# Xattn and six transformer layers on one core: two value stationaries per head, norm sums in SBUF, new slot orders

## Chip, cores and metric

The kernel runs on 1 core of one Trainium2 chip. The metric is device time in microseconds: the median of 3 runs.

## What is computed

Input x is 32 sequences of 128 tokens by 128 features, all fp32. First comes one cross attention (16 heads of 8, 4 key heads) with a residual. Then six layers of windowed attention and FFN, 192 pairs of (layer, sequence), which the kernel calls units. The part that the change is about, cut from the reference:

```python
def local_attention(q, k, v):          # 16 heads of 64, windows of 32
    bk2, bv2 = (look(bk), look(bv))    # each window sees the one before and itself
    mask = (it < jb) | (it > jb + w) | (jb == -1)
    sim = jnp.einsum('bhwie,bhwje->bhwij', bq, bk2) * QK_SCALE
    sim = jnp.where(mask, -jnp.finfo(sim.dtype).max, sim)
    attn = jax.nn.softmax(sim, -1)
    out = jnp.einsum('bhwij,bhwje->bhwie', attn, bv2)

def attn_layer(x, Wqkv, qs, ksc, Wo):
    q = l2norm(q) * qs; k = l2norm(k) * ksc      # per head
    q = q * cos * scale + rotate_half(q) * sin * scale
    k = k * cos * inv + rotate_half(k) * sin * inv
    return local_attention(q, k, v) @ Wo

def ffn_layer(x, g, bln, W1, b1, W2, b2):
    xn = (x - mu) / jnp.sqrt(var + 1e-05) * g + bln
    a, gate = jnp.split(xn @ W1 + b1, 2, -1)
    return a * gelu(gate) @ W2 + b2

for i in range(6):
    x = attn_layer(shift_tokens(x), ...) + x
    x = ffn_layer(shift_tokens(x), ...) + x
```

`shift_tokens` moves the second half of the features one token on.

## The kernel before, in words

Every engine runs its own program, written by hand as a list of steps with semaphore waits. The cross attention goes through 32 sequences in `xslot`. After that all engines go through `slot(n)`. In slot n TensorE, VectorE, ScalarE and GpSimd work on several units at once, each at its stage of the pipeline: unit n+2 is copied in, n+1 is transposed (`transpose_z`), unit n is projected to q, k and v and rotated, n-1 is normalized, n-2 has its heads transposed and its scores made, n-3 goes through softmax, P transposes and attend, n-4 through the output product (`attn_out`), the middle residual `z_mid`, the second norm and the first FFN product, n-5 through the last one. The order of the calls at the end of each engine's `slot` is the order of the work; there is no scheduler.

All data and products are fp32, so a product is two passes on TensorE (two instructions in the trace). The steps of TensorE in order: `attn_out` (L1363), `ffn_out` (L1351), `proj_qk(1)` (L1252), `transpose_qk` (L1290, 64 transposes of 32 rows), `transpose_z` (L1377), `proj_qk(2)` and `(3)`, `transpose_P` (L1270), `scores` (mask writes L1314, 64 products L1322), `attend` (48 products L1339), `transpose_zn` (L1383), `proj_v(0)` (L1262), `ffn_gate` (L1392), `ffn_a` (L1400), `proj_qk(0)`, `proj_v(1)`.

PSUM has eight banks. Banks 0 and 1 take the six projections of 512 columns in turn: each is squared and rotated (`rotary`, L963 and L966 on VectorE, into ta and tb) before the next may write. GpSimd adds ta and tb (L524) and multiplies by the norms rn (L533). Banks 2 to 5 take the head transposes; banks 2 and 3 (`SC`) also take the scores, and hold between them the sums of squares, the steps of the root (L976, L979, L982) and the row sums (L1075). So `transpose_qk` waits for `d_rn` (L985) and `d_rec`:

```python
wait(pe, "g_qk", count(4, b, 4))
wait(pe, "d_rn", count(1, m, 1))
wait(pe, "d_sub", count(2, b - 1, 2))
wait(pe, "d_rec", count(1, b - 1, 1))
```

Values are copied to vt (L705). The SP queue then makes the three overlapping shifts of them, vs, by DMA (`shift_v`, L351, six DMAs of a unit), and the one-token shift of zm (`shift_z`, L356). The statistics of the second norm (L1009) wait for that one. SP also loads the next layer's weights, in one fixed order. At the end of a layer this is `load_b2` (waits for the last zmb of GpSimd, L548), `shift_v(end + 2)`, `load_w1`, and then the first `shift_z` of the new layer.

## Time and profile before

| | |
|---|---|
| runs, us | 3307.62, 3308.11, 3310.73; median 3308.11 |
| profiled execution | span 3304.7 us (of this execution the span is what is known) |
| median less that span | 3.4 us |
| TensorE busy | 3125.4 us, 95% |
| VectorE, ScalarE, GpSimd busy | 87%, 81%, 74% |
| mean granted clock of TensorE | 0.978 |
| first transposed z of the layers | 302.3 us |
| last one | 3209.3 us |

The profile is of one execution. Busy time of TensorE overlaps, since a matmul's duration contains its way through the array; the distance between starts tells what a block costs. Idle time of an engine that nobody waits for costs nothing.

### The profile page before, as it was taken

The page shows a single profiled execution, that of the slowest core. Times are in us where ns is not written, and L with a number is a line of the kernel's source. Part 1 is how long each engine was busy: PE and PEld are TensorE (multiplying, and loading weights), DVE is VectorE, ACT ScalarE, POOL GpSimd, SP SyncE. Part 2 cuts the span into 40 slices and gives each one's busy share as a digit, 9 for nine tenths or more (in the row PEclk, how much of TensorE's full clock was granted, in tenths as well). Part 3 has the DMA queues.
Part 4 walks back from the last instruction along what each step waited for, and adds up shares of the span by engine and source line. Part 5 has one row for each costly group of instructions (what it writes and reads, how often), then busy time and mean ns, then how long its engine had stood idle before and what let it go on. Part 6 is the DMA issues. An engine that isn't in the chain of part 4 may idle for free.

```text
span 3304.7 us, 181505 instructions
## 1 busy us (share of the span) xinstructions
PE 3125.4 (95%) x71268; PEld 2192.5 (66%) x71268; DVE 2884.0 (87%) x6045; ACT 2663.4 (81%) x5440; POOL 2447.9 (74%) x2673
## 2 busy tenths in 40 slices
PE   6776899999999999999999999999999999999996
PEld 4443567676667676676767667676676767667665
DVE  7886789999899999899999899998899999899984
ACT  6886678888788888788888788888788888788874
POOL 3333778888788888788888778787787878788883
PEclk9988999999999999999999999999999999999997
DMA  3000112122222222222222212122221212212121
GB/s 79 8 7 10 47 51 59 50 59 71 67 56 53 56 53 77 63 54 55 54 55 74 68 50 59 50 59 77 57 59 50 59 50 77 66 50 59 50 58 50
DMA packets 150374, 182.24 MB, mean 55 GB/s; under 512 B 51572, under 2 KB 74162, under 8 KB 149554
## 3 DMA queue, kind: packets, MB, share of 16 engines
q1 hardware_dynamic: 150322, 181.55, 21.2%
q8 instruction: 33, 0.54, 0.1%
q14 instruction: 19, 0.16, 0.0%
HBM read 21.32 MB, written 2.10 MB: 7 GB/s over the span
## 4 chain that ended last, share of the span: by engine, by line
PE 57%; issue 13%; DVE 10%; ACT 10%; POOL 5%; SPq 1%; DVEq 1%; DMA 1%; ACTq 1%; POOLq 0%
PE bank L1252 13%; PE bank L1339 8%; PE bank L1322 7%; PE bank L1262 5%; PE bank L1363 5%; PE bank L1270 3%; PE bank L1290 3%; ACT L798 3%; DVE tb L966 3%; ACT P L774 3%; PE bank L1392 2%; ACT gl L766 2%; POOL qk L524 2%; DVE bank L1075 2%; PE bank L1400 2%
## 5 line engine op out<-in xcount | busy, mean ns | idle before, releaser
L533 POOL TENSOR_TENSOR qk<-qk,rn 128x512 f32<-128x512 f32 x768 | 803.0, 1046 | 356.8 <-DVE rn L985 356.8
L524 POOL TENSOR_TENSOR qk<-ta,tb 128x512 f32<-128x512 f32 x768 | 978.6, 1274 | 2.5 <-DVE tb L966 2.5
L1252 PE MATMUL bank<-wqkv,zsT 128*128 128x512 f32 x1536 | 819.9, 617 | 25.4 <-ACT vt L705 12.3
L963 DVE TENSOR_TENSOR ta<-bank,rot 128x512 f32<-128x512 f32 x768 | 527.5, 687 | 116.1 <-ACT sq L688 87.4
L966 DVE TENSOR_TENSOR tb<-bank,rot 128x512 f32<-128x512 f32 x768 | 523.0, 681 | 0.0
L1068 DVE TENSOR_REDUCE bank<-sq 128x32 f32<-128x2048 f32 x192 | 440.6, 2295 | 25.1
L688 ACT ACTIVATE sq<-bank 128x512 f32<-128x512 f32 x768 | 445.2, 611 | 14.8 <-PE bank L1252 12.1
L696 ACT ACTIVATE qkT<-bank 128x512 f32<-128x512 f32 x768 | 396.6, 602 | 57.1 <-PE bank L1290 56.9
L1363 PEld LDWEIGHTS bank<-wo,oT 128*128 128x128 f32 x3072 | 375.4, 193 | 92.4 <-issue 92.4
L743 ACT ACTIVATE znT<-bank,small 128x128 f32<-128x128 f32 x192 | 87.9, 458 | 431.8 <-PE bank L1383 431.8
L564 POOL TENSOR_TENSOR P<-P,rowsum 128x512 f32<-128x512 f32 x384 | 392.9, 1045 | 20.0 <-DVE rowsum L1083 20.0
L1262 PE MATMUL bank<-wqkv,zsT 128*128 128x512 f32 x768 | 399.8, 603 | 1.2 <-DVE tb L966 1.1
L1363 PE MATMUL bank<-wo,oT 128*128 128x128 f32 x3072 | 376.6, 276 | 0.5 <-ACT gl L766 0.5
L1252 PEld LDWEIGHTS bank<-wqkv,zsT 128*128 128x128 f32 x1536 | 238.0, 195 | 193.1 <-DVE tb L966 170.2
L1290 PEld LDWEIGHTS bank<-cst,qk 32*128 32x128 f32 x12288 | 212.5, 137 | 172.9 <-issue 172.9
L1339 PE MATMUL bank<-PT,vs 64*64 64x32 f32 (+1 forms) x18432 | 310.9, 220 | 11.3 <-issue 11.3
L1339 PEld LDWEIGHTS bank<-PT,vs 64*64 64x64 f32 x18432 | 291.4, 135 | 30.0 <-issue 12.3
L539 POOL TENSOR_TENSOR rstd<-ve,half_neg 128x1 f32<-128x1 f32 x192 | 105.8, 551 | 254.5 <-DVE ve L1023 254.5
L1075 DVE TENSOR_REDUCE bank<-P 128x16 f32<-128x1024 f32 x192 | 235.8, 1228 | 66.7 <-ACT P L774 66.6
L1322 PEld LDWEIGHTS bank<-qkT 64*32 64x32 f32 x24576 | 278.1, 105 | 14.1 <-issue 3.9
L1322 PE MATMUL bank<-qkT 64*32 64x64 f32 x24576 | 281.7, 225 | 3.0 <-issue 3.0
L1290 PE MATMUL bank<-cst,qk 32*128 32x32 f32 x12288 | 228.5, 223 | 21.0 <-DVE rowsum L1083 2.9
(131 smaller groups left out, 5740.6 us busy)
## 6 DMA issues: line engine op xcount, KB each, us to landing
vs<-vt SPq DMA_DIRECT2D x1152, 128.0 KB, 2.4
wqkv<-L_ffn_Wqkv SPq DMA_DIRECT2D x6, 1024.0 KB, 5.0
zm<-zm SPq DMA_DIRECT2D x192, 31.8 KB
wqkv<-L_ffn_Wqkv SPq DMA_DIRECT2D x6, 512.0 KB, 3.7
wo<-L_ffn_Wo SPq DMA_DIRECT2D x6, 512.0 KB, 4.0
z_sb<-x SPq DMA_DIRECT2D x4, 512.0 KB, 5.1
ctxb<-ctx SPq DMA_DIRECT2D x32, 64.0 KB, 1.8
w<-L_ffn_W SPq DMA_DIRECT2D x6, 341.0 KB
```

What stands on the lines that cost most here:

```text
L524: g.tensor_tensor(o, i0, i1, ALU.add).then_inc(s["g_add"], 1)
L533: g.tensor_tensor(q3, q3, r3, ALU.mult).then_inc(s["g_qk"], 1)
L688: a_.activation(sq[:, 512 * j:512 * j + 512], bank[j % 2][:, :], ACT.Square)\
L963: v_.tensor_tensor(ta[:, c].rearrange("p (h d) -> p h d", d=DH), bank[j % 2][:, :].rearrange("p (h d) -> p h d", d=DH), rot[:, o:o + 64].u ...
L966: v_.tensor_tensor(tb[:, c].rearrange("p (h c d) -> p h c d", c=2, d=32)[:, :, ::-1, :], bank[j % 2][:, :].rearrange("p (h c d) -> p h c d ...
L1068: v_.tensor_reduce(sm, sq[:, :].rearrange("p (h d) -> p h d", d=DH), AX.X, ALU.add)\
L1252: t_.matmul(bank[j % 2][:, :], zsT[:, pu, :], wqkv[:, 512 * j:512 * j + 512], start=True, stop=True).then_inc(s["p_qk"], 1)
L1262: t_.matmul(bank[r][:, :], zsT[:, k % 2, :], wv[:, :, r, :], start=True, stop=True)\
L1290: ins = t_.transpose(TB[t][:, 32 * p:32 * p + 32], qk[tok, pb, 128 * p:128 * p + 128], ident[tok, tok])
L1322: ins = t_.matmul(SC[e][32 * w:32 * w + 32, 64 * p:64 * p + 64], qkT[dr, p, 32 * w:32 * w + 32], qkT[dr, PAIRS + p, k0:k0 + 64], start=Fal ...
L1339: ins = t_.matmul(bank[4 + r][64 * e:64 * e + 64, 128 * i + q0:128 * i + q0 + nq], vs[kr, pc, w, hc:hc + 64], PT[kr, 4 * e + i, q0:q0 + nq ...
L1363: ins = t_.matmul(bank[7][:, 384:512], oT[:, p, :], wo[:, 2 * (p % 4) + p // 4, :], start=p == 0, stop=p == PAIRS - 1)
```

## The change

Semaphores. One counter per step and part (`d_rot0` to `d_rot3`, `g_qk0` to `g_qk3`, ...) takes the place of one counter per kind of step. Each engine's `slot` is written out anew, in another order, each step with its own lag behind n.

Attend. vs holds two stationaries of 64 keys in place of three. P's transposes go into PTA (96 query columns: 0 to 63, and 64 to 95 with one half of the keys zeroed) and PTC (64 columns: 64 to 95 with the other half zeroed, and 96 to 127), by four copies with a 0/1 scale. Two products per head add up in PSUM.

Scores. Windows 0 and 1 become one product of 64 query rows by 64 keys per head; windows 2 and 3 stay apart, with the two halves of window 2's keys swapped.

Norms. sm, n0, n1 and rs are in SBUF. The second norm (epsilon, rstd, zn) is on GpSimd. `z_mid` and the output product have lag 3, and stand near the end of the slot.

```diff
-        PT = sb("PT", [128, PAIRS, S])
+        PTA = sb("PTA", [128, PAIRS, 3 * WIN])
+        PTC = sb("PTC", [128, PAIRS, 2 * WIN])
-        vs = sb("vs", [128, 2, 3, INNER // 2])
+        vs = sb("vs", [128, 2, 2, INNER // 2])
+        sm = sb("sm", [128, 2 * HEADS])
+        n0 = sb("n0", [128, 2 * HEADS])
+        n1 = sb("n1", [128, 2 * HEADS])
+        rs = sb("rs", [128, HEADS])
...
-                for r in range(2):
-                    wait(sp, "a_v", count(2, u, r + 1))
+                for r in (1, 0):
+                    wait(sp, f"a_v{r}", done(u))
                     wait(sp, "p_AV", count(2, u - 2, 2))
-                    for j in range(3):
-                        sp.dma_start(vs[rows, par, j, :], vt[32 * j:32 * j + 64, par, r, :])...
+                    for j in range(2):
+                        sp.dma_start(vs[rows, par, j, :], vt[64 * j:64 * j + 64, par, r, :])...
...
+                u, on, p = unit(n, k, 4)          # GpSimd, first in its slot
+                    wait(pool, "d_agg", done(u))
+                    g.tensor_tensor(ve[:, p:p + 1], mv[:, 1:2], eps[:, 0:1], ALU.add)...
+                    g.tensor_tensor(rstd[:, p:p + 1], ve[:, p:p + 1], half_neg[:, 0:1], ALU.pow)...
+                    g.tensor_scalar(zn[:, :], zm[:, p, 0:2, :]..., mv[:, 0:1], rstd[:, p:p + 1],
+                                    ALU.subtract, ALU.mult).then_inc(s["d_zn"], 1)
...
+                    a_.activation(PTA[:, :, 64:96], bank[5]...[:, :, 0:32], ACT.Copy, scale=cst[:, C_HALF:C_HALF + 1])
+                    a_.activation(PTA[:, :, 0:64], bank[4]..., ACT.Copy)
+                    a_.activation(PTC[:, :, 32:64], bank[5]...[:, :, 32:64], ACT.Copy)
+                    a_.activation(PTC[:, :, 0:32], bank[5]...[:, :, 0:32], ACT.Copy, scale=cst[:, C_HALF + 1:C_HALF + 2])
...
-                        for p in range(PAIRS):
-                            for w in range(4):
-                                for e in range(2):
-                                    k0 = WIN * max(w - 1, 0)
-                                    ins = t_.matmul(SC[e][32 * w:32 * w + 32, 64 * p:64 * p + 64],
-                                                    qkT[dr, p, 32 * w:32 * w + 32], qkT[dr, PAIRS + p, k0:k0 + 64], ...)
+                    for c in range(PAIRS):
+                        for w in range(2, 4):
+                            for e in range(2):
+                                ins = t_.matmul(SC[e][32 * w:32 * w + 32, 64 * c:64 * c + 64],
+                                                qkT[dr, c, 32 * w:32 * w + 32], kb[:, ::-1, :] if w == 2 else kb, ...)
...
+                    for c in range(PAIRS):
+                        for e in range(2):
+                            ins = t_.matmul(SC[e][0:64, 64 * c:64 * c + 64], qkT[dr, c, 0:64], qkT[dr, PAIRS + c, 0:64], ...)
...
-                            for w, (q0, nq) in enumerate(((0, 64), (64, 32), (96, 32))):
-                                for r in range(2):
-                                    for e in range(2):
-                                        ins = t_.matmul(bank[4 + r][64 * e:64 * e + 64, 128 * i + q0:128 * i + q0 + nq],
-                                                        vs[kr, pc, w, hc:hc + 64], PT[kr, 4 * e + i, q0:q0 + nq], ...)
+                                ins = t_.matmul(bank[4 + r][64 * e:64 * e + 64, 128 * i + 0:128 * i + 96],
+                                                vs[kr, p, 0, hc:hc + 64], PTA[kr, 4 * e + i, :], ...)
...
+                                ins = t_.matmul(bank[4 + r][64 * e:64 * e + 64, 128 * i + 64:128 * i + 128],
+                                                vs[kr, p, 1, hc:hc + 64], PTC[kr, 4 * e + i, :], ...)
...
+                    wait(pe, "g_qk1", done(u))        # head transposes, with d_rn and d_rec gone
+                    wait(pe, "d_sub1", done(u - 1))
```

TensorE before, from the P transposes to the gate product in the loop (L1270 P transposes, L1314 masks, L1322 scores, L1339 attend, L1383 zn, L1262 a value projection, L1392 gate):

```order
L1270 MATMUL bank<-cst,P 128x64 x16
L1314 MATMUL bank<-maskb,selb 32x512 x8
L1322 MATMUL bank<-qkT 32x64 x64
L1339 MATMUL bank<-PT,vs 64x64 x4
L1339 MATMUL bank<-PT,vs 64x32 x8
...
L1383 MATMUL bank<-cst,zn 128x128
L1262 MATMUL bank<-wqkv,zsT 128x512
L1392 MATMUL bank<-znT,w 128x128 x2
```

TensorE of the change, from the same P transposes to the end of the slot (L1366 scores of windows 2 and 3, L1418 scores of windows 0 and 1, L1406 and L1436 attend, L1474 output product, L1502 head transposes; L1382, L1449, L1464, L1484 and L1510 are projections):

```order
L1343 MATMUL bank<-cst,P 128x64 x16
L1358 MATMUL bank<-maskb,selb 32x512 x8
L1366 MATMUL bank<-qkT 32x64 x32
L1375 MATMUL bank<-cst,zn 128x128
L1382 MATMUL bank<-wqkv,zsT 128x512
...
L1406 MATMUL bank<-PTA,vs 64x96 x16
L1418 MATMUL bank<-qkT 64x64 x16
L1436 MATMUL bank<-PTC,vs 64x64 x16
L1449 MATMUL bank<-wqkv,zsT 128x512
...
L1474 MATMUL bank<-wo,oT 128x128 x8
L1484 MATMUL bank<-wqkv,zsT 128x512
L1502 MATMUL bank<-cst,qk 128x32 x64
```

The scores stand in two places, with zn, a value projection and the gate product between them, and the second lies between the two halves of attend. The output product is behind them rather than at the slot's start, and the head transposes are almost last.

GpSimd of the change, from the start of its slot (L537 epsilon, L539 rstd, L546 zn, L553 the first add, L560 the first normalization, L566 the copy of the next input):

```order
L537 TENSOR_TENSOR ve<-mv,eps 128x1
L539 TENSOR_TENSOR rstd<-ve,half_neg 128x1
L546 TENSOR_SCALAR zn<-zm,mv,rstd 128x128
L553 TENSOR_TENSOR qk<-ta,tb 128x512
L560 TENSOR_TENSOR qk<-qk,rn 128x512
...
L566 COPY zcur<-z_sb 128x128
```

Before, rstd stood behind a normalization, two products of P and an add, and zn was VectorE's last step of a slot.

## Rows read from the trace of the kernel before

**Rows 1.** The page's head: span, and busy time by engine.
```profile
span 3304.7 us, 181505 instructions
PE 3125.4 (95%) x71268; PEld 2192.5 (66%) x71268; DVE 2884.0 (87%) x6045; ACT 2663.4 (81%) x5440; POOL 2447.9 (74%) x2673
```
**Rows 2.** The z transposes (L1377): duration, first and last start; all, then a stretch.
```profile
L1377 PEld LDWEIGHTS bank<-cst,zcur x192: 137/139/230, 302.3 to 3209.3; 128*128 128x128 f32 x192
L1377 PEld LDWEIGHTS bank<-cst,zcur x29: 137/139/140, 914.9 to 1335.6; 128*128 128x128 f32 x29
```
**Rows 3.** Timeline of TensorE in one slot: start, duration, engine, line.
```profile
1000.36 1.95 PE L1363 MATMUL bank<-wo,oT 128*128 128x128 f32 x16
1002.14 0.83 PE L1351 MATMUL bank<-w,hT 128*128 128x128 f32 x6
1002.81 1.02 PE L1252 MATMUL bank<-wqkv,zsT 128*128 128x512 f32 x2
1003.96 1.19 PE L1290 MATMUL bank<-cst,qk 32*128 32x32 f32 x64
...
1005.24 2.17 PE L1252 MATMUL bank<-wqkv,zsT 128*128 128x512 f32 x4
1007.34 0.71 PE L1270 MATMUL bank<-cst,P 64*128 64x64 f32 x16
...
1008.21 1.46 PE L1322 MATMUL bank<-qkT 64*32 64x64 f32 x128
1009.61 1.60 PE L1339 MATMUL bank<-PT,vs 64*64 64x64 f32 x96
1011.14 0.33 PE L1383 MATMUL bank<-cst,zn 128*128 128x128 f32 x1
...
1013.62 1.02 PE L1252 MATMUL bank<-wqkv,zsT 128*128 128x512 f32 x2
1014.49 1.02 PE L1262 MATMUL bank<-wqkv,zsT 128*128 128x512 f32 x2
```
**Rows 4.** Timeline of VectorE in the same slot.
```profile
1003.00 0.28 DVE L1001 TENSOR_TENSOR zm<-bank,z_sb 128x128 f32<-128x128 f32 x1
...
1003.46 0.15 DVE L985 SCALAR_TENSOR_TENSOR rn<-bank,rn 128x32 f32<-128x32 f32 x1
...
1005.55 0.68 DVE L966 TENSOR_TENSOR tb<-bank,rot 128x512 f32<-128x512 f32 x1
...
1006.71 0.30 DVE L1009 BATCH_NORM_STATS2 stats<-zm 128x6 f32<-128x128 f32 x1 [0.28 <-DMA zm<-zm]
1007.11 0.18 DVE L1017 BATCH_NORM_AGGREGATE mv<-stats 128x2 f32<-128x6 f32 x1
...
1010.19 0.61 DVE L1030 TENSOR_SCALAR zn<-zm,mv,rstd 128x128 f32<-128x128 f32 x1
```
**Rows 5.** One layer boundary: SP's timeline and VectorE's statistics.
```profile
861.71 0.34 SPq L341 DMA_DIRECT2D b2r<-L_ffn_b  x1
862.16 3.69 SPq L351 DMA_DIRECT2D vs<-vt  x6
865.90 0.58 SPq L329 DMA_DIRECT2D w<-L_ffn_W  x1
866.53 0.65 SPq L356 DMA_DIRECT2D zm<-zm  x1
...
870.76 0.29 DVE L1009 BATCH_NORM_STATS2 stats<-zm 128x6 f32<-128x128 f32 x1 [4.70 <-DMA zm<-zm]
```
**Rows 6.** Groups by line: busy, mean of one | idle before.
```profile
L1339 PE MATMUL bank<-PT,vs 64*64 64x32 f32 (+1 forms) x18432 | 310.9, 220 | 11.3 <-issue 11.3
L1322 PE MATMUL bank<-qkT 64*32 64x64 f32 x24576 | 281.7, 225 | 3.0 <-issue 3.0
L539 POOL TENSOR_TENSOR rstd<-ve,half_neg 128x1 f32<-128x1 f32 x192 | 105.8, 551 | 254.5 <-DVE ve L1023 254.5
L548 POOL TENSOR_TENSOR zmb<-zm,b2r 128x128 f32<-128x128 f32 x184 | 84.7, 460 | 0.0
```

More of the change, by code:

```diff
@@ new lines, in slot @@
+                    ins.then_inc(s["p_S23"], 1)
+                u, on, p = unit(n, k, 4)
+                if on:
+                    wait(pe, "d_zn", done(u))
+                    edge(pe, u, "z_ready", done(u - 1) + B if not (isinstance(u, int) and u - 1 < 0) else 0)
+                    t_.transpose(bank[6][:, 0:128], zn[:, :], ident).then_inc(s["p_znT"], 1)
+                u, on, p = unit(n, k, 0)
+                if on:
+                    wait(pe, "d_rot3", done(u))
+                    edge(pe, u, "a_zs", done(u))
+                    wait(pe, "l_wv", 16 * layer_of(u) + 16)
+                    t_.matmul(bank[1][:, :], zsT[:, p, :], wv[:, :, 1, :], start=True, stop=True).then_inc(s["p_v1"], 1)
@@ new lines, in slot @@
+                u, on, p = unit(n, k, 4)
+                if on:
+                    wait(pe, "a_zn", done(u))
+                    edge(pe, u, "a_zs", done(u + 5))
+                    wait(pe, "l_w1", 16 * layer_of(u) + 16)
+                    for j, (o, m_) in enumerate(FCH):
+                        ins = t_.matmul(bank[7][0:m_, 128 * j:128 * j + 128], w1[:, FF + o:FF + o + m_], znT[:, :], start=True, stop=True)
+                    ins.then_inc(s["p_gate"], 1)
+                u, on, p = unit(n, k, 3)
@@ new lines, in slot @@
+                u, on, p = unit(n, k, -1)
+                if on:
+                    wait(pe, "a_v1", done(u - 1))
+                    edge(pe, u, "a_zs", done(u))
+                    if isinstance(u, int) and u == 0:
+                        pe.wait_ge(s["x_add"], 4 * B)
+                    wait(pe, "l_wqk", 16 * layer_of(u) + 16)
+                    t_.matmul(bank[1][:, :], zsT[:, p, :], wqkv[:, 512:1024], start=True, stop=True).then_inc(s["p_qk1"], 1)
+                u, on, p = unit(n, k, 4)
@@ new lines, in slot @@
+                u, on, p = unit(n, k, 3)
+                if on:
+                    wait(pe, "a_AV0", done(u))
+                    edge(pe, u, "a_AV1", done(u))
+                    edge(pe, u, "a_zs", done(u + 4))
+                    edge(pe, u, "a_gelu", done(u - 1))
+                    wait(pe, "l_wo", 16 * layer_of(u) + 16)
+                    for c in range(PAIRS):
+                        ins = t_.matmul(bank[7][:, 384:512], oT[:, c, :], wo[:, 2 * (c % 4) + c // 4, :], start=c == 0, stop=c == PAIRS - 1)
+                    ins.then_inc(s["p_y"], 1)
@@ new lines, in slot @@
+                u, on, p = unit(n, k, -1)
+                if on:
+                    wait(pe, "a_v0", done(u - 1))
+                    edge(pe, u, "a_zs", done(u))
+                    if isinstance(u, int) and u == 0:
+                        pe.wait_ge(s["x_add"], 4 * B)
+                    wait(pe, "l_wqk", 16 * layer_of(u) + 16)
+                    t_.matmul(bank[0][:, :], zsT[:, p, :], wqkv[:, 0:512], start=True, stop=True).then_inc(s["p_qk0"], 1)
+                u, on, p = unit(n, k, 1)
@@ L1421, in _ @@
+                u, on, p = unit(n, k, -1)
+                if on:
+                    wait(pe, "d_rot1", done(u))
+                    edge(pe, u, "a_zs", done(u))
+                    wait(pe, "l_wqk", 16 * layer_of(u) + 16)
+                    t_.matmul(bank[1][:, :], zsT[:, p, :], wqkv[:, 1536:2048], start=True, stop=True).then_inc(s["p_qk3"], 1)
             slots(pe, slot, xslot)
```

956 lines of the change are left out of this document (497 added, 459 removed), and 6 rows, old and new, of the table names.

## The prediction, as recorded before the result was known

> **What bounds the kernel now.** I read the page's busy line first [rows 1]: TensorE is busy 95% of the span, VectorE 87%, ScalarE 81%, GpSimd 74%. The next question is where a slot's time goes. The transposes of z start every slot; their first and last start give the slot's length [rows 2]: 28 slots from 914.9 to 1335.6, that is 15.025 us each, and 191 slots from 302.3 to 3209.3, 2907.0 us in all. 191 times 15.025 is 2869.8, so 37 us of the loop lie in slots longer than the others. The 302 us before (cross attention) and the 95 us behind aren't touched in their work; I carry them over as they are.
>
> The timeline of TensorE in one slot [rows 3] is the table for the sum. The reader should take starts, not durations, since matmuls overlap. One 512 column projection costs 0.87 (1013.62 to 1014.49, two passes). Sixteen passes of 128 columns take 1.78, or 0.111 each, 0.87 ns for a column. Head transposes and the z transpose take 1.28, the P transposes with the mask writes 0.87, scores 1.40, attend 1.53, the FFN's last product 0.67. Two places hold more than that. The projection at 1002.81 should end at 3.68, but the head transposes begin at 3.96: 0.28 us idle. The two projections at 1005.24 should take 1.74 and take 2.10: 0.36.
>
> Both gaps have a releaser on VectorE [rows 4]. The head transposes write into the score banks, in which the norm statistics and row sums lie, so they wait for rn, done at 3.61. The third projection waits for the second rotary product, done at 6.23. So TensorE's own work bounds the slot, with 0.64 us of dependency waits in it, and the lines listing shows no other idle time of weight. One boundary between layers is in [rows 5]: the SP queue sends b2, six vs copies (3.69 us), w1, and only then at 866.53 the zm shift, whose input was ready about 862.6 in this slot. Statistics start at 870.76 after 4.70 us of idle time.
>
> **The change, part by part (per slot, unless said).**
>
> *Attend.* Now 96 passes, in 24 rounds over four 64x64 tiles. Busy 1.60 less one matmul's 0.22 [rows 3, 6] is 1.38 from first to last start, 0.060 a round; the remaining 0.15 of 1.53 is the break to the next block of another tile form. With two stationaries there are 8 rounds of 96 columns and 8 of 64. By columns these are 0.084 and 0.056. A round can't be shorter than now while it loads four weights of 64 columns, so I take 0.084 and 0.060: 1.15 instead of 1.38, **-0.23**. Bounds: 0.056 for the second kind (-0.26), or weight loads shown on top (the second rival).
>
> *Scores.* Now 128 passes on eight 64x32 tiles, 16 rounds: 1.46 - 0.23 = 1.23, 0.08 a round. The change splits them. Windows 2 and 3 use four tiles, and need 16 rounds all the same, because each tile still gets 8 head pairs times 2 passes. Windows 0 and 1 become one product of 64 rows per head, on two tiles, and again 16 rounds. There are 48 products instead of 64, but the rounds double. A round of 64 columns is at least 0.056 and at most today's 0.08; I take 0.058, between the columns' share and attend's 0.060, since fewer weights are loaded per round. 32 rounds are 1.86: **+0.62** (bounds +0.56 and +1.3). Instruction counts mislead here: fewer instructions, more time.
>
> *Breaks.* Two breaks of 0.15 stay two (behind the first scores, behind the last attend block). New is an entry into tiled work behind the gate product, between 0 and 0.15: I take **+0.08**. Between the three 64x64 blocks the form stays, so 0 (bound 0.15 each).
>
> *Waits of TensorE.* Statistics and row sums are in SBUF, so the head transposes no longer wait for rn. Projections 0 and 1 are rotated one slot ahead and lie apart. Walking the new order with today's durations, each operand is there before TensorE asks: rotary 3 at about 3.1 of the slot against 3.9, rotary 2 at 4.3 against 9.5, normalized heads at 11.3 against 13.3. Both waits go, except an entry of 0.08 before each tiled block: -(0.64 - 0.16) = **-0.48** (bounds 0 and -0.64).
>
> *Other engines, taken at nothing.* ScalarE gets four copies of PT for two: three of 256 columns, each at most today's 0.60. That is up to 1.2 more on an engine that is idle 19% of the time, about 2.8 us a slot; its waiting reader is the first attend block, behind the gate product, which covers it with 0.1 to 0.2 us. VectorE loses zn (0.61) and the epsilon add. GpSimd gains both; its idle time is 26%, 3.9 us a slot, and behind zn stand its adds, needed two microseconds later than they come. If that cover is gone, it is the first rival. SP issues four vs copies for six, 1.2 us less.
>
> Steady slot: -0.23 + 0.62 + 0.08 - 0.48 = -0.01, over 191 slots **-2 us**.
>
> *Boundaries.* z_mid moves from the slot's start (lag 4) to its end (lag 3). b2, vs and w1, which stand ahead of that zm shift in SP's queue, are released by the residual, the attend and the first FFN product, all earlier in the same slot than the output product. So zm goes out when ready and only shares the DMA engines with w1. I take 1.0 us of the 4.70 as left: five times -3.7 is **-18.5 us** (bounds 0 and -25). The wo load stands right ahead of another zm shift now too, with no idle time shown; no gain or loss.
>
> Sum: -20.5 us. Against the profiled span 3304.7 this is 3284.2; the median of the runs is 3.4 us above that span (what lies around it), so 3287.6, say **3287 us**. A measurement of this kernel can tell about 0.2% from no change, 6.6 us.
>
> **One rule weighed.** GpSimd's elementwise work: the row shows 0.46 for a 128x128 add with two inputs on GpSimd [rows 6], and 0.61 for the very zn that moves, on VectorE [rows 4]. I therefore take 0.46 for zn on GpSimd. The Trainium skill, GPSIMD Engine Reference, section Key points, says that VectorE is structurally about twice as fast for elementwise work. By that rule zn would go from 0.61 to 1.22, which is the first rival; the trace speaks against it so far.
>
> **Rivals.**
>
> *1. The norm chain on GpSimd becomes the bound (slower).* From the output product to the znT transpose: zm to statistics 3.71 (1003.00 to 1006.71), statistics 0.30, then z_out 0.28 (as zm, of the same form), rn 0.15 and aggregate 0.18 ahead on VectorE [rows 4], epsilon add about 0.25 (less than the 0.55 of rstd), rstd 0.55, zn 0.46, and 0.6 for six handovers of about 0.1: 6.5 us. TensorE's work in between: two projections 1.74, head transposes and z transpose 1.28, FFN product 0.67, projection 0.87, P transposes and masks 0.87, first scores 0.93, break 0.15, entries 0.16: 6.7. The cover is 0.2 us. It decides as soon as the chain passes 6.7. At twice VectorE's own 0.61 zn is 1.22, the chain 7.2, TensorE waits 0.5 a slot, 191 times is 96 us: **3383**. For it: the thin cover, and a DMA in the chain. Against it: 0.46 in the row.
>
> *2. Weight loads show in the tiled blocks (slower).* 16 transposes with 128 column weights in two row groups took 0.71 - 0.23 over 7 steps, 0.07 a load, so about 0.03 for 64 columns and 0.015 for 32. If each round shows its load: 16 x 0.03 in attend, 16 x 0.03 and 16 x 0.015 in the scores, 1.2 a slot, 229 us: **3516**. Half of them: 3400. For it: scores at 0.08 a round instead of 0.056. Against it: attend's 0.060, and 0.111 for full passes, whose loads are wholly hidden. The Trainium skill, TensorE: Matmul & The Clock Gate, Part 3, says that a load overlaps a running matmul only in another row group; the full passes here differ from that.
>
> *3. The waits move, and the boundaries stay (no change).* Each dependency wait removed leaves another of its size, or zm still comes late behind w1: **3306**.
>
> *4. More is gained (faster).* Entries and breaks vanish too and the long first slots shrink: -0.2 a slot: **3245**.
>
> **How the numbers follow.** Forecast 0.45 (of it 0.43 faster, 0.02 within 0.2%), rival 1 0.20, rival 2 0.13, rival 3 0.12 (0.11 within, 0.01 slower), rival 4 0.10. Faster 0.53, same 0.13, slower 0.34. The range goes from 3240, short of rival 4, to 3400, past rival 1 and to the half of rival 2. Both signs hold much of the chance; the forecast's own range is 3262 to 3301.
>
> **What would show it.** Slot length near 15.0 with TensorE's blocks at about 1.15 for attend and 1.86 for scores; head transposes right behind their projection; zm shifts issued within a microsecond of zm. Rival 1 is right if znT waits for GpSimd's zn; rival 2 if a round of the tiled blocks takes over 0.09; rival 3 if statistics still idle over 4 us at boundaries. I am wrong altogether if an engine other than TensorE has no idle time in a slot.

## The result and the profile after

The changed kernel takes 3358.9 us (median of 4 runs, 3355.7 to 3359.1) against 3307.9 for the kernel before on the same chip: ratio 1.0156, 95% interval 1.0141 to 1.0170. It is slower by 51 us. The forecast was 3287, so the sign was wrong; the time lies in the range, and the first rival (3383) is what happened.

The page's head of the kernel after, which answers to [rows 1]:

```profile
span 3357.3 us, 146312 instructions
PE 3152.6 (94%) x58980; PEld 2231.6 (66%) x58980; DVE 2903.7 (86%) x5661; ACT 2850.6 (85%) x5827; POOL 2638.7 (79%) x3059
```

TensorE issues 12288 matmuls less (58980 for 71268), and the span is 52.6 us longer. The z transposes (now L1314), all and then a stretch, answer to [rows 2]:

```profile
L1314 PEld LDWEIGHTS bank<-cst,zcur x192: 138/142/180, 306.3 to 3264.4; 128*128 128x128 f32 x192
L1314 PEld LDWEIGHTS bank<-cst,zcur x29: 140/141/142, 902.0 to 1336.3; 128*128 128x128 f32 x29
```

Those are the first numbers to take. 28 slots from 902.0 to 1336.3 are 15.51 us each, 0.49 more than before; 191 times 0.49 is +93. The whole loop, 306.3 to 3264.4, is 2958.1 for 2907.0, so +51: slots that aren't steady (the first ones, and one or two at each layer's end) give 42 back. The loop starts 4.0 later and the tail is 2.5 shorter. Two large terms of opposite sign are behind the 51 us. Within the stretch the slots alternate between 15.265 and 15.76. (Those of the kernel before alternate too, between 14.93 and 15.12; the forecast had used only their mean.)

The timeline of TensorE in one of the shorter slots answers to [rows 3] (start, duration, engine, line, and in brackets idle time and its releaser):

```profile
1009.18 1.19 PE L1502 MATMUL bank<-cst,qk 32*128 32x32 f32 x64
1010.30 1.13 PE L1510 MATMUL bank<-wqkv,zsT 128*128 128x512 f32 x2
1011.26 0.27 PE L1314 MATMUL bank<-cst,zcur 128*128 128x128 f32 x1
...
1013.87 1.06 PE L1366 MATMUL bank<-qkT 64*32 64x64 f32 x64
1015.14 0.33 PE L1375 MATMUL bank<-cst,zn 128*128 128x128 f32 x1 [0.21 <-POOL zn L546]
...
1017.01 0.89 PE L1406 MATMUL bank<-PTA,vs 64*64 64x96 f32 x32
1017.72 1.03 PE L1418 MATMUL bank<-qkT 64*64 64x64 f32 x29
...
1018.65 0.64 PE L1436 MATMUL bank<-PTC,vs 64*64 64x64 f32 x30
```

Everything else stands close together; one place waits. The transpose of zn (L1375) has its bank and its place, and the operand isn't there. Of the list of waits of 28 slots (total, times, longest):

```profile
PEld bank L1375 <- POOL zn L546: 15.5, 28, 0.8
```

The matmul behind that weight load waits for zn too. Read by starts, and with 0.15 for the break behind the last score, znT (the transpose of zn) is 0.27 late in the shorter slots and 0.65 in the longer ones, 0.46 on average, and a slot of 15.51 without it would be 15.05: almost what it was before. The longest entry of that list is 44.2 us of GpSimd waiting for the row sums. No engine waits by semaphore for the products behind it, but they aren't free of the chain: the second one ends at 1012.57 (below), and the step n1 of VectorE, which stands ahead of the statistics, ends 0.06 behind it. The last section tells why.

The chain that ends in zn, on VectorE, in the same slot; it answers to [rows 4]:

```profile
1008.73 0.29 DVE L1137 TENSOR_TENSOR zm<-bank,z_sb 128x128 f32<-128x128 f32 x1 [0.50 <-PE bank L1474]
...
1011.49 0.18 DVE L1168 SCALAR_TENSOR_TENSOR n<-sm,rn 128x32 f32<-128x32 f32 x1
1011.71 0.92 DVE L1173 TENSOR_TENSOR n<-n,rn 128x32 f32<-128x32 f32 x1
1012.55 0.28 DVE L1178 BATCH_NORM_STATS2 stats<-zm 128x6 f32<-128x128 f32 x1
1012.75 0.27 DVE L1025 TENSOR_TENSOR z_sb<-bank,zmb 128x128 f32 x1
...
1013.04 0.17 DVE L1037 BATCH_NORM_AGGREGATE mv<-stats 128x2 f32<-128x6 f32 x1
```

and on GpSimd:

```profile
1011.51 1.06 POOL L617 TENSOR_TENSOR P<-P,rowsum 128x512 f32<-128x512 f32 x1
...
1013.29 0.19 POOL L537 TENSOR_TENSOR ve<-mv,eps 128x1 f32<-128x1 f32 x1 [0.30 <-DVE mv L1037]
1013.56 0.56 POOL L539 TENSOR_TENSOR rstd<-ve,half_neg 128x1 f32<-128x1 f32 x1
1014.29 0.80 POOL L546 TENSOR_SCALAR zn<-zm,mv,rstd 128x128 f32<-128x128 f32 x1 [0.18 <-POOL rstd L539]
```

From the output product's end (1006.44 + 1.95 = 1008.39) to znT (1015.14) is 6.75 us, of which 6.42 run from zm's start. TensorE has 6.48 of other work behind that end. In every second slot one more piece stands in this chain, ahead of z_sb (VectorE):

```profile
1028.37 0.29 DVE L1025 TENSOR_TENSOR z_sb<-bank,zmb 128x128 f32 x1 [0.39 <-issue]
```

"issue" is idle time that no semaphore ended; a body of the loop is two slots long, and this is its seam. From zm's start to znT are 6.90 us in these slots.

The boundary, which answers to [rows 5] (SP, then the residual and the statistics behind it):

```profile
866.86 0.53 SPq L352 DMA_DIRECT2D w<-L_ffn_W  x1
869.14 0.65 SPq L379 DMA_DIRECT2D zm<-zm  x1
...
868.82 0.29 DVE L1137 TENSOR_TENSOR zm<-bank,z_sb 128x128 f32<-128x128 f32 x1 [0.28 <-PE bank L1474]
872.63 0.28 DVE L1178 BATCH_NORM_STATS2 stats<-zm 128x6 f32<-128x128 f32 x1
```

zm goes out as soon as it is ready (868.82 + 0.29 = 869.11), and the statistics don't idle (4.70 before). That is the other large term. Counted from the starts of the z transposes, with the twelve slots around each boundary set against steady ones, the five boundaries cost 30.5 us before and 5.9 now. The first twelve slots of the layers, 5.7 us over steady ones before, are 10.1 us below them now. The two together are 40 of the 42 us.

### The profile page after: what moved, and what is told of

Its sections match the earlier page's. It is cut to its first block and busy times, and to the rows that moved or that the text cites. A ratio compares the mean times of both kernels' runs of the same rounds, so it can differ in the third digit from the quotient of the medians.

```text
span 3357.3 us, 146312 instructions
## 1 busy us (share of the span) xinstructions
PE 3152.6 (94%) x58980; PEld 2231.6 (66%) x58980; DVE 2903.7 (86%) x5661; ACT 2850.6 (85%) x5827; POOL 2638.7 (79%) x3059
## 5 line engine op out<-in xcount | busy, mean ns | idle before, releaser
L611 POOL TENSOR_TENSOR P<-P,rowsum 128x512 f32<-128x512 f32 x192 | 200.2, 1043 | 307.9 <-DVE rowsum L1150 307.9
L1072 DVE TENSOR_REDUCE sm<-sq 128x32 f32<-128x2048 f32 x192 | 436.2, 2272 | 0.0
L1474 PEld LDWEIGHTS bank<-wo,oT 128*128 128x128 f32 x3072 | 372.9, 192 | 92.1 <-issue 89.8
L1474 PE MATMUL bank<-wo,oT 128*128 128x128 f32 x3072 | 374.2, 275 | 1.0 <-ACT oT L802 1.0
L1078 DVE TENSOR_REDUCE rowmax<-bank 128x8 f32<-128x512 f32 x192 | 132.7, 691 | 214.3 <-PE bank L1418 214.3
L1502 PEld LDWEIGHTS bank<-cst,qk 32*128 32x128 f32 x12288 | 206.5, 137 | 144.5 <-issue 144.4
L553 POOL TENSOR_TENSOR qk<-ta,tb 128x512 f32<-128x512 f32 x192 | 244.2, 1272 | 3.3 <-DVE tb L1160 3.3
L1143 DVE TENSOR_REDUCE rs<-P 128x16 f32<-128x1024 f32 x192 | 232.0, 1209 | 0.0
L1502 PE MATMUL bank<-cst,qk 32*128 32x32 f32 x12288 | 227.7, 223 | 0.2 <-POOL qk L599 0.2
L1390 PEld LDWEIGHTS bank<-znT,w 128*128 128x128 f32 (+1 forms) x1152 | 138.2, 181 | 132.4 <-issue 68.3
L1449 PE MATMUL bank<-wqkv,zsT 128*128 128x512 f32 x384 | 218.0, 650 | 3.6 <-ACT zsT L740 2.2
L1510 PE MATMUL bank<-wqkv,zsT 128*128 128x512 f32 x384 | 216.0, 644 | 0.3 <-DVE tb L1127 0.3
L1418 PE MATMUL bank<-qkT 64*64 64x64 f32 x6144 | 212.4, 218 | 0.0
L1456 PEld LDWEIGHTS bank<-znT,w 128*128 128x128 f32 (+1 forms) x1152 | 151.5, 180 | 89.8 <-issue 89.5
L1343 PEld LDWEIGHTS bank<-cst,P 64*128 64x128 f32 x3072 | 110.8, 139 | 150.9 <-issue 150.9
L828 ACT ACTIVATE vt<-bank 128x512 f32<-128x512 f32 x192 | 114.6, 597 | 112.4 <-PE bank L1464 112.4
## 6 DMA issues: line engine op xcount, KB each, us to landing
zm<-zm SPq DMA_DIRECT2D x192, 31.8 KB
```

The lines of the kernel that those rows point to most:

```text
L553: g.tensor_tensor(qk[:, p, 0:512], ta[:, 0:512], tb[:, 0:512], ALU.add).then_inc(s["g_add0"], 1)
L1072: v_.tensor_reduce(sm[:, :], sq[:, :].rearrange("p (h d) -> p h d", d=DH), AX.X, ALU.add).then_inc(s["d_sumsq"], 1)
L1143: v_.tensor_reduce(rs[:, :], P[:, p, :].rearrange("p (h t) -> p h t", t=DH), AX.X, ALU.add).then_inc(s["d_sum"], 1)
L1449: t_.matmul(bank[1][:, :], zsT[:, p, :], wqkv[:, 512:1024], start=True, stop=True).then_inc(s["p_qk1"], 1)
L1474: ins = t_.matmul(bank[7][:, 384:512], oT[:, c, :], wo[:, 2 * (c % 4) + c // 4, :], start=c == 0, stop=c == PAIRS - 1)
L1502: ins = t_.transpose(TB[t][:, 32 * c:32 * c + 32], qk[tok, p, 128 * c:128 * c + 128], ident[tok, tok])
```

## The experiments

Theory after the result: the slot is set by the loop through the second norm, output product, zm, shift DMA, statistics, aggregate, rstd, zn, znT, since the scores' split left too little TensorE work beside it. Rivals: TensorE's own blocks are longer than booked (weight loads, entries, breaks), or another engine bounds. Times below are medians; the ratio is always to the kernel before on the same chip. That kernel took 3303.8 to 3307.9 us on the chips used, so a difference between two runs in microseconds is good to some 4 us.

### Four kernels on the chain

**no_shift** takes the DMA out of the chain: it leaves out the token shift ahead of the FFN.

```diff
-                sp.dma_start(zm[1:128, par, 1, :], zm[0:127, par, 2, :])...
+                sp.dma_start(zjunk[1:128, par, :], zm[0:127, par, 2, :])...
-                    wait(dve, f"l_s{p}", ...)        # ahead of bn_stats
+                    wait(dve, "d_zm", done(u))
```

> The DMA of the zm shift writes a spare tile, and the statistics and zn read zeros for the shifted half, so they do not wait for it (the token shift ahead of the FFN is left out). Theory A (the chain from the output product over zm, the shift's DMA, statistics and GpSimd's zn ends last at the znT transpose): 3.3 us leave the chain, znT stops waiting, slot 15.51 to about 15.05 us, total 3359 to about 3271 us. Theory B (TensorE's own work is longer, the wait before znT is only where it shows): no change, 3359 +- 7 us.

Measured: 3316.2 us, ratio 1.0038 [1.0023, 1.0052], 43 us less than the change, slots 15.40 and 15.28; 3271 was expected. The chain itself isn't shorter. n1 still takes 0.92 (1004.47 to 1005.39), and the statistics start behind it, 3.82 us behind zm's start as in the change (VectorE, a slot with the seam):

```profile
1020.59 0.28 DVE L1182 BATCH_NORM_STATS2 stats<-zm 128x6 f32<-128x128 f32 x1
1020.79 0.27 DVE L1028 TENSOR_TENSOR z_sb<-bank,zmb 128x128 f32 x1
```

What has gone is the idle time of the seam: z_sb stands 0.20 behind the statistics in every slot, and from zm's start to znT are 6.42 us in every slot, as in the change's shorter ones. The trace has VectorE's branch at 1027.71 in the change, level with the statistics that wait for the DMA (1027.70), and at 1019.84 here, beside n1 and 0.75 ahead of them. So 0.17 a slot, 32 us, is the seam's; 6 us more are at the boundaries, and the chain without its transfer is as long as with it.

**n1_one_port** changes the form of the two small norm steps (n1, and the maximum of sm), to see if the form makes n1 long.

```diff
-                    v_.tensor_tensor(n1[:, :], n0[:, :], rn[:, p, :], ALU.mult)...
+                    v_.scalar_tensor_tensor(n1[:, :], n0[:, :], 1.0, rn[:, p, :], ALU.mult, ALU.mult)...
```

> n1 and the maximum of sm become scalar_tensor_tensor instructions instead of tensor_tensor. If the 0.92 us of n1 (0.19 us before the change, when one input was in PSUM) is a wait for GpSimd's instruction in that form alone, n1 falls to about 0.2 us. Theory A with the DMA right behind: statistics can start only 0.12 us earlier, because the shift lands then, total about 3338 us. Rival (n1's wait is the whole overrun): slot 15.05, total 3271 us. Theory B: no change.

Measured: 3357.5 us, 1.0161 [1.0144, 1.0178], where 3338 was expected; n1 still takes 0.92. The form isn't it.

**aggr_early** puts the aggregate right behind the statistics, ahead of the seam.

```diff
                     v_.bn_stats(...).then_inc(s["d_bn"], 1)
+                    wait(dve, "d_bn", done(u))
+                    v_.bn_aggr(mv[:, :], stats[:, 0:6]).then_inc(s["d_agg"], 1)
-                    v_.bn_aggr(mv[:, :], stats[:, 0:6])...       # behind z_sb and rn, in the next slot
```

> bn_aggr directly behind bn_stats at the slot's end, ahead of z_out and rn (with real waits where the old order had implied them). Theory A: even slots gain about 0.15 us, odd slots about 0.6 us (the loop's branch on VectorE leaves the chain), both near 15.1 us, total about 3285 us. Theory B: no change.

Measured: 3315.2 us, 1.0029 [1.0018, 1.0041], 44 us less. The slots are 15.27 and 15.305: the short ones are what they were, the long ones have lost 0.45. So the seam was nearly the whole alternation, 0.22 on average, and this run and no_shift gain by the same thing. The 3285 expected counted on the short slots too. There zn ends only 0.07 earlier, and znT stands 0.13 behind its end rather than 0.06, with a wait more ahead of it.

**n_late** is aggr_early with n0 and n1 behind the aggregate, where GpSimd runs no product of P.

> The changed kernel with the aggregate right behind the statistics (alone: 3315 us, slot 15.29), and with the two steps of the norm root (n0, n1) behind them instead of ahead. GpSimd then runs no product of P beside them but epsilon and rstd of one column. My theory: a VectorE instruction with both inputs in SBUF stands until GpSimd's running one is over; n1 then takes at most 0.4 instead of 0.92, statistics start when zm lands, and the slot is about 0.1 shorter, 3296 us. Rival: n1 costs 0.92 wherever it stands: then z_out and rn come 0.9 later, and the time is 3315 or above. A transfer of zm that lands later than n1 ended before leaves the time at 3315 with n1 short.

Measured: 3345.9 us, 1.0116 [1.0099, 1.0133]. n1 is short now, 0.20. But its 0.92 had filled VectorE's wait for the DMA, and now VectorE idles there (one slot, below) and does the steps afterwards. The statistics start 3.44 us behind zm's end here, where only the DMA holds them, and 3.53 in the change, behind n1: the two branches end within 0.1 us. That is why neither no_shift nor this run shortens the chain by more than 0.1.

```profile
1009.60 0.29 DVE L1161 BATCH_NORM_STATS2 stats<-zm 128x6 f32<-128x128 f32 x1 [0.88 <-DMA zm<-zm]
```

The slot is 15.49, since VectorE's later steps are late: in one of two slots zm starts 0.66 behind the output product's end (0.34 in the change), in the other the projection behind znT waits for a rotary product, 0.37 more from start to start. The expectation got the duration right and the time wrong: a shorter instruction isn't a shorter chain where two branches end together.

**chain_cut** is all three at once (no_shift, aggr_early, n_late), so it leaves out the same token shift.

> The changed kernel with three pieces of the chain out of it at once: no transfer between the middle residual and the statistics (the token shift ahead of the FFN is left out, statistics and norm read zeros in that half), the statistics and the aggregate ahead of n0 and n1, the aggregate right behind the statistics. The chain is then about 1 us shorter than with either edit alone. Theory: znT no longer waits for zn, the slot is the sum of TensorE's blocks, 15.05, and the time about 3270 us. Rival: TensorE's other waits take the place of znT's (rowmax, row sums, P), the slot stays at 15.3 and the time at 3315.

Measured: 3265.6 us, 0.9879 [0.9863, 0.9896], slots 15.00 and 15.125. From the transposes of z:

```profile
L1315 PEld LDWEIGHTS bank<-cst,zcur x30: 140/140/142, 903.3 to 1340.0; 128*128 128x128 f32 x30
```

29 slots in 436.7 us, 15.06 each. This is the block sum of 15.05; znT is 0.03 late at most. Against the kernel before, the steady slots cost 0.03 each, 6 us, and the others give back 39; 6 us more lie behind the last z transpose. So of the 0.49 a slot 0.45 is the chain: 0.22 is the seam in it, the rest is what the DMA and n1 hold side by side, and only with both gone does it go. That TensorE's own blocks set the 15.51 is excluded.

### What the split of the scores costs

**scores_whole** puts all four windows into one block where windows 2 and 3 stand; the second block of scores is gone.

```diff
-                        for w in range(2, 4):
+                        for w in range(4):
...
-                    for c in range(PAIRS):
-                        for e in range(2):
-                            ins = t_.matmul(SC[e][0:64, 64 * c:64 * c + 64], qkT[dr, c, 0:64], ...)
```

> All four windows' scores in one block of 64 products where windows 2 and 3 stand, none between the halves of attend. Theory A: TensorE loses 0.82 us and gains about 0.39 us of work, and those 0.39 us lie between the output product and znT, so the wait there shrinks too: slot about 14.75 us, total about 3214 us. Theory B (work alone counts): -0.43 us a slot, about 3277 us. If merged windows 0 and 1 are cheaper than two apart: slower than 3359 us.

Measured: 3273.7 us, 0.9912 [0.9896, 0.9929]: 85 us less than the change, and faster than the kernel before. The 3214 expected was missed; the rival, which counted TensorE's work alone, had 3277. The block takes 1.24 from first to last start for 0.85 + 0.82, and it stands in the chain's cover, so znT waits in every second slot only. A new gap has come (TensorE):

```profile
1010.22 0.33 PE L1376 MATMUL bank<-cst,zn 128*128 128x128 f32 x1 [0.19 <-POOL zn L546]
...
1012.20 0.89 PE L1407 MATMUL bank<-PTA,vs 64*64 64x96 f32 x32
1013.27 0.69 PE L1426 MATMUL bank<-PTC,vs 64*64 64x64 f32 x32 [0.18 <-PE bank L1407]
```

The second half of attend starts 1.07 after the first, for 0.71: it waits for TensorE's own semaphore of the first half, which the scores between them used to cover.

**pair** is scores_whole without that wait, since the second half follows the first in TensorE's own program, and takes aggr_early with it.

```diff
-                    wait(pe, "p_AV0", done(u))
```

> The changed kernel with three edits together: the scores of all four windows in one block where those of windows 2 and 3 stand; no wait of its own between the two halves of attend, which now follow each other; the aggregate right behind the statistics. With the scores whole alone the slot was 15.05, with a wait of 0.26 before znT in every second slot and a gap of 0.36 more between the halves of attend. My theory: both are waits and nothing else bounds, so the slot becomes 15.05 - 0.36 - 0.13 = 14.56 and the time about 3180 us. Rival: the gap between the halves is the wait for ScalarE's last copies of P's transposes and comes back as a wait before the first half or inside it, then only znT's 0.13 goes: 3250 us. Rival 2: VectorE or GpSimd bounds below 15.0: then the time stays near 3270 and TensorE idles somewhere else.

Measured: 3203.7 us, 0.9687 [0.9671, 0.9703], the fastest kernel of the study. The wait between the halves is gone (0.71 from start to start), and the list of waits shows znT's no more:

```profile
1018.35 0.89 PE L1404 MATMUL bank<-PTA,vs 64*64 64x96 f32 x32
1019.06 0.64 PE L1422 MATMUL bank<-PTC,vs 64*64 64x64 f32 x32
```

By starts znT is still 0.13 late in the shorter slots and 0.08 in the longer ones, too little for that list. The short slots are 14.57 as expected, but partly by chance: about as much as znT's 0.13 went elsewhere, 0.05 of it behind attend. Every second slot is 14.86, so the time is 24 us above the 3180. In those, two projections that wait for VectorE's rotary products cost 0.19 more each, and 0.09 less lies elsewhere.

### The block behind a tiled block

In the changed kernel a projection right behind attend or the head transposes takes 0.96 to the next start rather than 0.86. **pa_first** puts the FFN's products ahead of it, **pair_pa** does so on pair.

```diff
+                    ... t_.matmul(bank[6]..., w1[:, o:o + m_], znT[:, :], ...)  # p_a, now first
                     ... next q/k projection into bank 1
-                    ... t_.matmul(bank[6]..., w1[:, o:o + m_], znT[:, :], ...)
```

> The changed kernel, only with the first FFN product ahead of the next q/k projection. Theory of the late second pass: projection 0.86 instead of 0.96, -0.10 a slot, 3340 us; the chain of the second norm, which sets the slot, starts 0.1 earlier as well since the block between znT and the output product is shorter. Rival: the next block pays it: 3359 us. If the rotary of that projection then comes too late for GpSimd's add, slower than 3359.

> As the kernel called pair, with the first FFN product (two products of 128 columns) ahead of the next q/k projection, so that this projection no longer follows a tiled block directly. Theory that a full projection's second pass is 0.10 late when it comes right behind a tiled block: this one takes 0.86 instead of 0.96 and the slot is 0.10 shorter, 19 us. Rival: whatever stands there first pays it, no change beyond 3 us.

Measured: 3355.7 us, 1.0149 [1.0132, 1.0166], and 3205.6 us, 0.9695 [0.9679, 0.9711]: both within 0.1% of their parents. The projection is at 0.86 now, and the FFN products take 0.77 for 0.66. Of the two kinds of block tried, the one that stands behind the tiled block pays 0.10.

### Parts of the change, alone on the kernel before

**b_sbuf**: sums and row sums in SBUF, the head transposes without their waits for them.

```diff
-                ym, sm, n0, n1, rs = rn[:, pm, :], SC[0][:, 0:32], SC[0][:, 32:64], SC[0][:, 64:96], SC[1][:, 0:16]
+                ym, sm, n0, n1, rs = rn[:, pm, :], sm_[:, :], n0_[:, :], n1_[:, :], rs_[:, :]
-                        wait(pe, "d_rn", count(1, m, 1))
-                        wait(pe, "d_rec", count(1, b - 1, 1))
```

> The kernel before with this one part of the change: sums of squares, root steps and row sums in SBUF, and the head transposes without their waits for rn and the row sums' reciprocal. If that wait was 0.28 us a slot of TensorE's path, as forecast: 191 x 0.28 = 53 us less, 3308 to about 3255 us. Rival: another operand is as late (the normalized heads, or the third projection's rotary product): no change.

Measured: 3304.6 us, 0.9993 [0.9983, 1.0002]. Of the 53 us expected none came. The gap ahead of the head transposes falls from 0.28 to 0.09, and it comes back before the next bank is free of the rotation (TensorE):

```profile
1010.27 2.32 PE L1256 MATMUL bank<-wqkv,zsT 128*128 128x512 f32 x4
1012.52 0.71 PE L1274 MATMUL bank<-cst,P 64*128 64x64 f32 x16
```

The four passes hold 2.25 here; before they hold 2.10 in the slot of [rows 3] and 2.23 in the other kind. Over both kinds the head transposes win 0.17, and the four passes and the z transpose ahead of them lose 0.15. What the first wait gave up, the second took: that one is for VectorE's rotation, and VectorE has not become faster.

**b_bound**: only the order in SP's queue, w1 and the zm shift ahead of the vs copies.

```diff
                     load_b2(layer + 1)
-                    shift_v(end + 2, 0)
                     load_w1(layer + 1)
...
                 shift_z(start, 0)
                 if layer > 0:
+                    shift_v(start + 2, 0)
```

> The kernel before with only SP's order changed at a layer's end: w1 right behind b2, then the first zm shift of the new layer, and the six vs copies of unit end+2 behind it. Forecast's account of the boundaries: zm goes out about 862.7 instead of 866.5, statistics' 4.7 us of idle time shrink to about 1, five times: 3308 to about 3288 us. Rival: vs or w1 is then late and the time comes back: no change.

Measured: 3279.3 us, 0.9926 [0.9909, 0.9943], -25 us where -20 was expected. SP at the boundary, where zm goes out 3 us earlier than in [rows 5]:

```profile
862.90 0.42 SPq L329 DMA_DIRECT2D w<-L_ffn_W  x1
863.58 0.64 SPq L356 DMA_DIRECT2D zm<-zm  x1
864.33 4.97 SPq L351 DMA_DIRECT2D vs<-vt  x6
```

**b_two_st**: only the two stationaries, with their copies of P's transposes.

> The kernel before with only the two value stationaries (PTA, PTC, two copies of vs; scores stay four windows in one block, window 2's keys swapped). Forecast: attend 1.38 to 1.15 us between first and last start, slot -0.23 us, 3308 to about 3264 us. Rival 2 of the prediction (weight loads show): attend 1.6 us, 3320 us. Rival: the four copies on ScalarE make attend wait: a gap ahead of attend, no gain.

Measured: 3282.5 us, 0.9932 [0.9915, 0.9948], -22 us for the -44 expected. Attend takes 1.14 from its first to its last start; TensorE's stretch:

```profile
1001.14 1.46 PE L1334 MATMUL bank<-qkT 64*32 64x64 f32 x128
1002.71 0.89 PE L1351 MATMUL bank<-PTA,vs 64*64 64x96 f32 x32
1003.39 0.67 PE L1351 MATMUL bank<-PTC,vs 64*64 64x64 f32 x32
```

Scores to attend are 1.57 instead of 1.40, since attend waits for ScalarE's copies, and the steady slot stays at 15.01. So the gain isn't in attend. About half of the 22 us is at the boundaries: four copies stand ahead of zm in SP's queue instead of six, and slots of 20.3 to 21.7 become 18.0 to 19.2. The steady slots are 0.02 shorter, 4 us, the first ones of the layers give 3, and the rest lies behind the last z transpose, in work that wasn't traced further.

**zn_dve**: the changed kernel with zn on VectorE, behind the first pair of rotations.

> The changed kernel with zn back on VectorE, behind the first rotary pair of its slot. Theory A: zn ends 0.15 to 0.2 us earlier (0.61 us behind rstd and the rotary pair, against 0.80 us and a gap of 0.18 us on GpSimd), so the slot goes from 15.51 to about 15.35 us and the total from 3359 to about 3327 us. Rival: GpSimd was not the matter, VectorE is the fuller engine: no change or slower.

Measured: 3408.5 us, 1.0317 [1.0300, 1.0334], 50 us slower still, where 3327 was expected. zn on VectorE, all of them and one, the GpSimd product beside it, and then TensorE:

```profile
L1048 DVE TENSOR_SCALAR zn<-zm,mv,rstd x192: 345/1094/1130, 377.5 to 3396.0; 128x128 f32<-128x128 f32 x192
```

```profile
1009.88 0.94 DVE L1048 TENSOR_SCALAR zn<-zm,mv,rstd 128x128 f32<-128x128 f32 x1
```

```profile
1009.47 1.27 POOL L545 TENSOR_TENSOR qk<-ta,tb 128x512 f32<-128x512 f32 x1
```

```profile
1010.88 0.33 PE L1374 MATMUL bank<-cst,zn 128*128 128x128 f32 x1 [0.90 <-DVE zn L1048]
```

zn ends at 1010.82 and GpSimd's add at 1010.74. Of the 192 zn, 189 end 0.08 or 0.09 behind a GpSimd instruction that ran when they began; the three that had none beside them took 0.35. GpSimd was the better place, in spite of the 0.80.

### The seam of the loop

**unroll4** and **pair_u4** have four slots in the body in place of two.

```diff
-        LOOP0, UNROLL = 8, 2
+        LOOP0, UNROLL = 10, 4
```

> The changed kernel with four slots instead of two in the body of the loop, nothing else. Theory: of the alternating slots 15.265 and 15.76 the longer one holds 0.49 of the engines' branch and register work, which stands in the chain of the second norm ahead of z_out; with four slots per branch only one in four is long, the mean is 15.39 instead of 15.51, and the time about 3336 us. Rival: the alternation comes from the two halves of the buffers or from another cause of period two: the slots stay 15.27 and 15.76, 3359 us. Rival 2: the longer program has its instructions fetched later: slower than 3359.

> The fastest version so far (pair, 3204 us, slots 14.57 and 14.86) with four slots in the loop's body. Theory: the 0.29 of the longer slot is the branch again, one in four remains long, mean 14.64 instead of 14.72: 3190 us. Rival: a period of two that is not the branch: 3204 us.

Measured: 3626.1 us, 1.0976 [1.0958, 1.0995], and 3612.3 us, 1.0937 [1.0919, 1.0956]. Six transposes of z ahead of the loop, where no seam is, and from the page the instruction queue (packets, MB, share):

```profile
L1314 PEld LDWEIGHTS bank<-cst,zcur x6: 140/140/142, 387.6 to 464.1; 128*128 128x128 f32 x6
```

```profile
q8 instruction: 571, 9.36, 1.0%
```

The five straight slots are 15.30 each, without alternation: the same as aggr_early, and again 0.21 below the change's mean. In the loop two slots of four are 15.15, the other two 18.2 and 19.6, with TensorE idle by "issue":

```profile
938.81 0.47 PE L1314 MATMUL bank<-cst,zcur 128*128 128x128 f32 x1 [2.66 <-issue]
```

The packets of the instruction queue are 9.36 MB instead of the 0.54 of the two-slot body. The likely reading is that a body of four slots is fetched anew in every turn; the trace shows the traffic and the idle time, not a limit. Rival 2 of unroll4's expectation came, and far larger than thought. pair_u4's time therefore can't tell whether pair's 0.29 in every second slot is the seam. Its trace speaks for it: the two undisturbed slots of a body are 14.64 and 14.67, without the alternation.

## Why the prediction was wrong, by its steps

- **The step that failed** is "Other engines, taken at nothing", with "behind zn stand its adds, needed two microseconds later than they come. If that cover is gone, it is the first rival". The cover was gone. The rival gave the chain 6.5 and its cover 6.7; measured in the shorter slots are 6.75 and 6.48. On the chain's side the 0.46 for zn was mis-sized: it is 0.80 (192 of 192), and 0.18 lies between rstd and zn on one engine, where 0.1 was booked. An add of two tensors was no model for an operation with two per-partition scalars. The other links came out 0.15 shorter in sum. On the cover's side TensorE's work was summed well (6.67 booked, 6.64 measured), but from the next block's start, and the chain can only begin at the output product's end, 0.16 later. The rule that I set against it, twice VectorE's time by the Trainium skill, GPSIMD Engine Reference, section Key points, gives 1.22, and 0.80 was measured. But the 0.61 of [rows 4] was itself no pure VectorE time. Of the kernel before, all zn on VectorE, and the GpSimd product beside the one in [rows 4]:

```profile
L1030 DVE TENSOR_SCALAR zn<-zm,mv,rstd x192: 467/610/1056, 382.2 to 3295.0; 128x128 f32<-128x128 f32 x192
```

```profile
1009.68 1.04 POOL L533 TENSOR_TENSOR qk<-qk,rn 128x512 f32<-128x512 f32 x1
```

All 192 end 0.08 or 0.09 behind the GpSimd instruction beside them, whether they take 0.47, 0.61 or 1.06. The three that stood alone in zn_dve took 0.35, and 0.80 is 2.3 times that: set against that time the rule comes near the trace. Rival 1 had TensorE wait 0.5 a slot and it waits 0.46, but that is partly luck, since the rival took 1.22 for zn and knew nothing of the seam.
- **Not in the sum at all**: the seam of the loop. With lag 3, z_mid and its statistics stand at a slot's end and the aggregate at the next one's start, so what VectorE does between two bodies came into the chain: 0.22 a slot on average, 42 us (aggr_early, no_shift, unroll4's straight slots). The kernel before has a seam too, 0.17 of idle time on VectorE ahead of a rotation, and its slots alternate by 0.19: TensorE waits 0.13 longer at the third projection and 0.06 at the head transposes.
- **Also unseen**: n1 at 0.92. It ends with the DMA, within 0.1 us, so shortening it alone gains nothing (n_late), and taking out the DMA alone gains nothing in the chain either (no_shift). GpSimd's products of P hold n1, so a second branch of the chain runs from zm over the row sums and GpSimd to the statistics.
- **Attend** was right: 1.13 for 1.15. **Scores** were booked at 1.86 and measured 1.67: +0.44 rather than +0.62 a slot.
- **Waits** were booked at -0.48. The 0.28 ahead of the head transposes and the 0.36 ahead of the third projection behave as one wait with two places, so moving the sums to SBUF gains nothing alone (b_sbuf). In the new order both are gone and the sum -0.01 holds: 15.05 without znT's wait (chain_cut 15.06) for 15.025. Part of it was luck, since projections and FFN products behind tiled blocks cost 0.10 more than booked, twice a slot, where I had put 0.
- **Boundaries** were booked at -18.5 and measured -25 (30.5 to 5.9). The mechanism was right (b_bound: -25 for the queue's order alone). The first slots of the layers give 16 more, which I had left at zero; why is open.
- **Rival 2**, weight loads showing, is dead as a cost of the change: a round of 64 columns takes 0.057 in the split scores (0.85 over 15 steps) and 0.061 in attend (0.43 over 7), and one of 96 columns 0.093 (0.65 over 7), against 0.056 and 0.084 by columns. The 0.093 is over the 0.09 that was named as the sign, but the excess over the columns is about 0.1 us a slot, not 1.2. Rounds on eight tiles stay at 0.083 for 64 columns (scores_whole, as before); no run tells why. By the Trainium skill, TensorE: Matmul & The Clock Gate, Part 3, a load overlaps a running matmul only in another row group. The full passes of the change, 0.111 from start to start with a load each, show none of it.

With 0.20 on rival 1 against 0.45 on the forecast the chance was misplaced as well: a cover of 0.2 us, from sums of seventeen terms in all, each uncertain by some hundredths, should have had near even odds.

## What to carry to other kernels

When a step moves to another engine, add up its whole chain against the work that covers it, with the duration of the same operation form, not of one that looks alike, and look what runs beside the row that you take; a cover of a few tenths is none. Put no part of a critical chain on both sides of the loop's seam. Count rounds per tile rather than instructions: 64 products on eight small tiles (1.24) beat 48 on four and two (1.67), and the block left whole was also the cover that the chain needed. Test a part alone before crediting it, since two waits in a row may be one. And when an edit gains, look in the trace for the link that became shorter: no_shift gained 43 us, and its chain from zm to znT was as long as before.

## What the runs showed of the hardware

A VectorE instruction with both inputs in SBUF that begins beside a running GpSimd instruction ends only when that one is over. Of the 128x32 product n1, all 192, in the change, in n_late and in b_sbuf (ns: shortest, median, longest):

```profile
L1173 DVE TENSOR_TENSOR n<-n,rn x192: 191/918/1260, 330.9 to 3293.4; 128x32 f32<-128x32 f32 x192
```

```profile
L1175 DVE TENSOR_TENSOR n<-n,rn x192: 191/199/1265, 330.4 to 3288.6; 128x32 f32<-128x32 f32 x192
```

```profile
L986 DVE TENSOR_TENSOR n_<-n_,rn x192: 178/180/192, 333.0 to 3243.9; 128x32 f32<-128x32 f32 x192
```

In b_sbuf GpSimd is idle at that place. In the change n1 ends at 1012.63 and GpSimd's product of P at 1012.57; 190 of the 192 end 0.03 to 0.07 us behind the GpSimd instruction beside them. In chain_cut the same pairing shows twice. Of the first, n0 on VectorE and then GpSimd:

```profile
1009.87 0.60 DVE L1174 SCALAR_TENSOR_TENSOR n<-sm,rn 128x32 f32<-128x32 f32 x1
```

```profile
1009.39 1.04 POOL L620 TENSOR_TENSOR P<-P,rowsum 128x512 f32<-128x512 f32 x1
```

The ends are 1010.47 and 1010.43. Those of n1 and GpSimd's next step, zmb, are 1010.89 and 1010.85. The Trainium skill states this in SBUF — State Buffer, section "SBUF: two separate sides": a VectorE operation with two SBUF inputs and a GpSimd operation that reads SBUF take one port pair in turn, each for its whole length. The trace agrees. The zn of VectorE, with one tensor and two columns as inputs, is held in the same way (kernel before and zn_dve, above). So moving small tensors from PSUM to SBUF, as this change does, can make a 0.18 us step 0.92.

Also: a projection or a pair of FFN products that follows a tiled block on TensorE takes 0.10 more (pa_first), and the zm shift, 31.8 KB in one transfer, takes 3.4 us from zm's end to the statistics (n_late), half of the norm's chain.
